# From the first block to the second attention: a first token block sent ahead, bias and gate rows issued sooner, value products and later blocks moved

## The reference

```python
# layer 0, feed-forward: one expert pair for the whole sequence
pooled = ln(x).mean(axis=1)
gate = softmax(pooled @ gate_w.T); top_w, top_i = top_k(gate, 2); top_w /= top_w.sum() + 1e-8
h = gelu(ln(x) @ down_w[top_i].T + down_b[top_i]) * top_w
x = x + h @ up_w[top_i] + (top_w * up_b[top_i]).sum()
# layer 1, attention over 64 anchors, 16 heads of 64
a    = softmax(ln(x) @ W_qk.T @ W_anchor.T / 8)          # tokens x 16 x 64
out  = (a.T @ v) / a.sum(tokens)                         # 16 x 64 x 64
x    = x + (a @ out) @ W_out.T + b_out
```

## Time and profile before

| | |
|---|---|
| runs, median (lowest, highest) | 721.29 us (720.11, 721.71) |
| the profiled execution | 719.99 us, span 718.3 us |
| TensorE busy share, mean granted clock | 97 %, 0.999 |
| VectorE, GpSimd, ScalarE busy share | 81 %, 78 %, 64 % |
| stages around the change, us from the span's start | feed-forward 0 some 475 to 500, attention 1 some 501 to 576 |

### The profile page before, as it was taken

One profiled execution on the slowest core, in us unless ns is written; L12 is line 12 of the kernel. 1 busy time (PEld: TensorE's weight loads), 2 busy tenths in 40 slices (PEclk: granted clock), 3 DMA queues, 4 the chain that ended last, 5 costly groups with the idle time before them and its releaser, 6 DMA issues.

```text
span 718.3 us, 12481 instructions
## 1 busy us (share of the span) xinstructions
PE 698.3 (97%) x4280; PEld 470.6 (66%) x4280; DVE 582.4 (81%) x1213; ACT 460.3 (64%) x1069; POOL 563.6 (78%) x466
## 2 busy tenths in 40 slices
PE   8999999999999999999999999999899999999997
PEld 7665556566566566566666656476566599778885
DVE  8878888988988898898889888756978536878885
ACT  4357776776776777767767766655677822465553
POOL 6468999999999999999999997415688761446674
PEclk9999999999999999999999999999999999999999
DMA  6313768778678688687687683040000000032431
GB/s 152 93 38 67 146 126 155 132 137 151 124 148 150 116 154 153 113 156 146 121 153 139 133 155 67 1 121 2 1 2 0 2 1 1 1 89 81 141 104 30
DMA packets 42595, 68.34 MB, mean 95 GB/s; under 512 B 14872, under 2 KB 24105, under 8 KB 38692
## 3 DMA queue, kind: packets, MB, share of 16 engines
q0 software_dynamic: 15680, 52.96, 38.8%
q1 hardware_dynamic: 25572, 14.47, 7.6%
q10 hardware_dynamic: 1280, 0.12, 0.1%
HBM read 13.35 MB, written 1.10 MB: 20 GB/s over the span
## 4 chain that ended last, share of the span: by engine, by line
PE 71%; POOL 11%; issue 7%; DVE 7%; DMA 3%; ACT 2%; POOLq 0%; ACTq 0%; DVEq 0%
PE ps L1540 16%; PE ps L1584 15%; PE ps L1526 15%; POOL hid_lo L1055 5%; PE ps L1953 4%; PE ps L1568 4%; POOL nrm L1035 2%; DVE mx L1109 2%; PE ps L1993 2%; PE ps L1995 2%; PE ps L1994 2%; POOL hid L1035 1%; DMA w_v<-prob 1%; PE ps L1604 1%; PE ps L1513 1%
## 5 line engine op out<-in xcount | busy, mean ns | idle before, releaser
L1109 DVE TENSOR_REDUCE mx<-ps 128x1 f32<-128x512 f32 x492 | 303.1, 682 | 47.9 <-PE ps L1526 47.8
L658 ACT ACTIVATE prob<-ps 128x512 f32<-128x512 f32 x512 | 261.8, 627 | 21.3 <-PE ps L1540 16.2
L1540 PE MATMUL ps<-q_cols,key 128*128 128x512 f32 x512 | 210.3, 414 | 2.3 <-ACT prob L658 1.7
L1526 PE MATMUL ps<-key,q_rows 128*128 128x512 f32 x512 | 202.8, 400 | 0.8 <-DVE key L1095 0.4
L1540 PEld LDWEIGHTS ps<-q_cols,key 128*128 128x128 f32 x512 | 95.4, 187 | 73.9 <-issue 34.1
L1584 PE MATMUL ps<-prob,val 128*32 128x512 f32 x1024 | 123.3, 598 | 0.0
L1526 PEld LDWEIGHTS ps<-key,q_rows 128*128 128x128 f32 x512 | 95.7, 188 | 18.8 <-DVE mx L1103 1.4
L960 POOL TENSOR_TENSOR pair<-prob 128x512 f32<-128x512 f32 x60 | 104.8, 1770 | 4.0 <-ACT prob L658 4.0
L946 POOL TENSOR_TENSOR part<-prob 128x512 f32<-128x512 f32 x64 | 96.5, 1820 | 5.7 <-ACT prob L658 5.6
L1055 POOL TENSOR_TENSOR hid_lo<-hid,hid_hi 128x512 fp32r<-128x512 f32 x44 | 61.6, 1409 | 38.6 <-ACT hid_hi L826 38.6
L1584 PEld LDWEIGHTS ps<-prob,val 128*32 128x32 f32 x1024 | 26.7, 109 | 51.1 <-issue 47.4
(11 more groups left out here) (301 smaller groups left out, 1319.4 us busy)
## 6 DMA issues: line engine op xcount, KB each, us to landing
part<-prob POOLq DMA_DIRECT2D x16, 1024.0 KB, 7.1
part<-part POOLq DMA_DIRECT2D x14, 512.0 KB, 8.1
w_v<-prob POOLq DMA_DIRECT2D x7, 1024.0 KB, 7.1
hn<-prob POOLq DMA_DIRECT2D x7, 1024.0 KB, 7.0
part<-part POOLq DMA_DIRECT2D x14, 256.0 KB, 7.4
w_v<-w_v POOLq DMA_DIRECT2D x7, 512.0 KB, 8.0
hn<-hn POOLq DMA_DIRECT2D x7, 512.0 KB, 8.0
g_all<-g_rows SPq DMA_DIRECT2D x9, 256.0 KB, 3.2
```

The source lines that it names most:

```text
L658: act.activation(prob[:, g % RING, :], ps[:, g % 3, :], ACT.Exp, scale=SCALE).then_inc(s_exp, 1)
L1109: dve.tensor_reduce(mx[:, n % 2, c % TPB, at:at + 1], ps[:, BANK["rows", 2 * lin + j], :], AX.X, ALU.max).then_inc(s_mrd, 1)
L1526: pe.matmul(ps[:, BANK["rows", 2 * lin + j], :], q_rows[:, k, i * P:(i + 1) * P], key[:, h % KBUF, c0:c0 + BLK], start=True, stop=True).th ...
L1540: pe.matmul(ps[:, g % 3, :], key[:, n // NB % KBUF, t * P:(t + 1) * P], q_cols[:, n % NB, :], start=True, stop=True).then_inc(s_sc, 1)
```

## The change

On PE the group of 8 idle products ahead of the pooled sum is replaced by `values1(0)` and `values1(1)`; the group r = 2 takes the place that r = 0 had between the gate products, and r = 3 stands behind `hidden(3)`. The products for the gate row and for `top_w` are issued ahead of `hidden(0)`, that for the bias row right behind it, and `hidden(1)` goes behind `up(0)`. `ln1_T(0)` goes ahead of `up(2)`, and `up(3)`, `ln1_T(1)` and `ln1_T(2)` go into the loop. ACT copies `top_w` where DVE did, copies `bias0` before it scales `sel_uT`, and makes `ln1_norm(2)`, `ln1_act(1)` and so on inside the loop's turns. DVE normalises block 0 right behind its statistics, and takes `stream0(3)` and the subtractions of blocks 1, 2 and 3 behind turns 0, 1 and 2. POOL's list is as before, and so are the semaphores that the u = 0 slot waits for.

```diff
-        V_BANK = (1, 3, 2, 3)
+        V_BANK = (3, 1, 2, 3)
-        AT_TW = D + E
+        AT_TW = P + 2 * C
@@ ScalarE @@
                 anchors_hi(1)
+                values1(0)
+                values1(1)
                 act.wait_ge(s_gv, 2)
...
                 ln0_act(act, 3, 4)
+                values1(2)
                 act.wait_ge(s_sd_ps, 1)
                 act.copy(sel_dT[:, :], ps[:, 3, 0:P]).then_inc(s_sdT, 1)
-                values1(0)
                 act.wait_ge(s_gb_ps, 1)
                 act.copy(gb[:, :], ps[0:E, 0, AT_GB:AT_GB + P]).then_inc(s_gbc, 1)
+                act.copy(top_w[:, :], ps[:, 0, AT_TW:AT_TW + 1]).then_inc(s_tw, 1)
                 act.wait_ge(s_selb, 1)
                 hidden(0)
+                act.wait_ge(s_b0_ps, 1)
+                act.copy(bias0[:, :], ps[:, 0, AT_BIAS:AT_BIAS + D]).then_inc(s_b0, 1)
+                act.wait_ge(s_su_ps, 2)
                 act.wait_ge(s_tw, 1)
                 act.activation(sel_uT[:, :], ps[:, 2, 0:D], ACT.Copy, scale=top_w[:, :]).then_inc(s_suT, 1)
-                act.wait_ge(s_b0_ps, 1)
-                act.copy(bias0[:, :], ps[:, 0, AT_BIAS:AT_BIAS + D]).then_inc(s_b0, 1)
                 hidden(1)
                 hidden(2)
                 hidden(3)
+                values1(3)
+                ln1_act(act, 0, T1_BANK[0])
                 act.activation(warm[:, :], ones_row[:, 0:1], ACT.Exp)
-                values1(1)
-                ln1_act(act, 0, T1_BANK[0])
                 ln1_norm(act, 1)
-                values1(2)
-                ln1_act(act, 1, T1_BANK[1])
-                ln1_norm(act, 2)
-                values1(3)
-                ln1_act(act, 2, T1_BANK[2])
                 for t in range(NT + LAG1):
                     if t == 1:
+                        ln1_norm(act, 2)
+                        ln1_act(act, 1, T1_BANK[1])
+                    elif t == 2:
                         ln1_norm(act, 3)
-                    elif t == 2:
+                        ln1_act(act, 2, T1_BANK[2])
+                    elif t == 3:
                         ln1_act(act, 3, T1_BANK[3])
@@ VectorE @@
                 anchors_lo(0)
-                dve.wait_ge(s_tw_ps, 2)
-                dve.tensor_copy(top_w[:, :], ps[:, 2, AT_TW:AT_TW + 1]).then_inc(s_tw, 1)
                 anchors_lo(1)
                 stream0(0)
+                ln1_norm(dve, 0)
                 stream0(1)
-                ln1_norm(dve, 0)
+                ln1_lo(dve, 0, T1_BANK[0])
                 stream0(2)
-                ln1_lo(dve, 0, T1_BANK[0])
-                stream0(3)
-                ln1_lo(dve, 1, T1_BANK[1])
...
-                    if t == 1:
+                    if t == 0:
+                        stream0(3)
+                    elif t == 1:
+                        ln1_lo(dve, 1, T1_BANK[1])
+                    elif t == 2:
                         ln1_lo(dve, 2, T1_BANK[2])
                         ln1_lo(dve, 3, T1_BANK[3])
@@ TensorE @@
                 anchor_weights(1)
-                spin(8, 6)
+                pe.wait_ge(s_wo, 2)
+                pe.wait_ge(ln0["hT"], NB + 3)
+                values1(0)
+                values1(1)
                 pe.wait_ge(ln0["hn"], 2 * NT)
...
                 ln0_pe(pe, 3, 4)
-                pe.wait_ge(s_wo, 2)
-                value(0, 0)
-                value(0, 1)
+                value(2, 0)
+                value(2, 1)
...
-                value(0, 2)
-                value(0, 3).then_inc(s_wv_ps, 1)
+                value(2, 2)
+                value(2, 3).then_inc(s_wv_ps, 1)
                 spin(2, 6)
-                pe.wait_ge(ln0["hT"], NB + 3)
+                pe.wait_ge(s_wv, 1)
...
                 last.then_inc(s_sd_ps, 1)
+                pe.wait_ge(s_wv, 3)
...
                 last.then_inc(s_su_ps, 1)
+                pe.wait_ge(s_gv, 10)
+                pe.matmul(ps[0:E, 0, AT_GB:AT_GB + P], g8[:, IDX, :], ones_row[:, :], start=True, stop=True)
+                for k in range(2):
+                    last = pe.matmul(ps[k * BN:(k + 1) * BN, 0, AT_TW:AT_TW + 1], ones_row[:, 0:BN], g1[:, 5 + k:6 + k], start=True, stop=True)
+                last.then_inc(s_gb_ps, 1)
                 pe.wait_ge(s_sdT, 1)
                 hidden(0)
+                pe.wait_ge(s_tw, 1)
+                pe.matmul(ps[:, 0, AT_BIAS:AT_BIAS + D], gb[:, :], up0_b[:, :], start=True, stop=True).then_inc(s_b0_ps, 1)
                 pe.wait_ge(s_selb, 1)
                 pe.wait_ge(s_upx, 1)
...
+                last.then_inc(s_su_ps, 1)
-                hidden(1)
                 pe.wait_ge(s_suT, 1)
                 up(0)
+                hidden(1)
                 hidden(2)
                 up(1)
                 hidden(3)
-                values1(1)
+                values1(3)
+                ln1_T(0)
                 up(2)
-                ln1_T(0)
-                up(3)
-                values1(2)
-                ln1_T(1)
-                pe.wait_ge(s_wv, 1)
                 pe.wait_ge(s_b0, 1)
                 for t in range(NT + LAG1):
                     if t == 1:
-                        values1(3)
+                        up(3)
+                        pe.wait_ge(s_wv, 4)
+                    elif t == 2:
+                        ln1_T(1)
                         ln1_T(2)
-                        pe.wait_ge(s_wv, 4)
                     elif t == 3:
                         ln1_T(3)
```

More of the change, by code:

```diff
@@ L387, in build_kernel @@
         s_oh_ps, s_pick, s_sd_ps, s_sdT, s_su_ps, s_suT, s_selb = (sem(n) for n in ("s_oh_ps", "s_pick", "s_sd_ps", "s_sdT", "s_su_ps", "s_suT", "s_selb"))
-        s_tw_ps, s_tw, s_gb_ps, s_gbc, s_b0_ps, s_b0, s_xb = (sem(n) for n in ("s_tw_ps", "s_tw", "s_gb_ps", "s_gbc", "s_b0_ps", "s_b0", "s_xb"))
+        s_tw, s_gb_ps, s_gbc, s_b0_ps, s_b0, s_xb = (sem(n) for n in ("s_tw", "s_gb_ps", "s_gbc", "s_b0_ps", "s_b0", "s_xb"))
         s_h0_ps, s_h0, s_y0_ps, s_x2 = sem("s_h0_ps"), sem("s_h0"), sem("s_y0_ps"), sem("s_x2")
@@ L1798, in values1 @@
                 def values1(r):
[L1800 to L1805, removed]
                     for q in range(4):
@@ L1870, in _ @@
                 last.then_inc(s_su_ps, 1)
+                pe.wait_ge(s_gv, 10)
[3 more added lines that the diff above has]
+                last.then_inc(s_gb_ps, 1)
                 pe.wait_ge(s_sdT, 1)
                 hidden(0)
-                pe.wait_ge(s_gv, 10)
-                pe.matmul(ps[0:E, 0, AT_GB:AT_GB + P], g8[:, IDX, :], ones_row[:, :], start=True, stop=True).then_inc(s_gb_ps, 1)
+                pe.wait_ge(s_tw, 1)
+                pe.matmul(ps[:, 0, AT_BIAS:AT_BIAS + D], gb[:, :], up0_b[:, :], start=True, stop=True).then_inc(s_b0_ps, 1)
                 pe.wait_ge(s_selb, 1)
@@ L1878, in _ @@
                     last = pe.matmul(ps[:, 2, 0:D], masks[j], up_x[:, j, :], start=(j == 0), stop=(j == E // 2 - 1))
-                for k in range(2):
-                    pe.matmul(ps[k * BN:(k + 1) * BN, 2, AT_TW:AT_TW + 1], ones_row[:, 0:BN], g1[:, 5 + k:6 + k], start=True, stop=True).then_inc(s_tw_ps, 1)
-                hidden(1)
-                pe.wait_ge(s_gbc, 1)
-                pe.matmul(ps[:, 0, AT_BIAS:AT_BIAS + D], gb[:, :], up0_b[:, :], start=True, stop=True).then_inc(s_b0_ps, 1)
+                last.then_inc(s_su_ps, 1)
                 pe.wait_ge(s_suT, 1)
                 up(0)
+                hidden(1)
                 hidden(2)
```

## The result

| | before | changed |
|---|---|---|
| median of 7 runs each (lowest, highest) | 720.44 us (719.39, 721.93) | 723.15 us (722.7, 724.56) |
| ratio, 95 % interval | | 1.0033 (1.0017 to 1.005) |
| span of the profiled execution | 718.3 us | 721.0 us |
| mean granted clock of PE, profiled execution | 0.999 | 0.995 |

The kernel became slower by 0.2 to 0.5 %: 2.4 us by the ratio, 2.7 by the two medians and by the two profiled executions. The forecast was +1.9, and 723.2 us for the median. Behind the numbers that agree stand other parts: +1.1 comes from the new order, less than forecast, and +1.65 from PE's clock, a rival that the prediction had given 6 in 100.

The account below looks back on a forecast made before the run. PE hardly waits from tile 1's slot (517.65) on, so only that start counts; the parts moved it to 519.6, +1.95, tile 2 +1.9. On the median, 721.29 + 1.9 = 723.2 us; 8-in-10 range 720.6 to 725.2.

Parts of the forecast that it names:

- Part 1: Value products replacing PE's spins: pooled sum and gate search start 0.40 us later, bounds 0 and 0.8.
- Part 2: Gate and bias rows: bias row 1.6 us sooner, DVE's add only 0.7 us sooner, bounds 0.3 and 1.1.
- Part 3: DVE normalising block 0 at once: stands still 1.45 us, then meets POOL's bias add; ends 496.83 instead of 497.55.
- Part 4: Into the loop: late half sum and lo of blocks 2 and 3 put tile 0's slot at 515.55, not 511.52.
- The sum: Tile 1's slot 4.04 us behind tile 0's, at 519.6 against 517.65; +1.9 us on the whole kernel.
- the three gaps: PE idle some 7 us in all, ahead of `ln1_T(2)`, `ln1_T(3)` and the slot of tile 0.
- (a): Rival: same order, without the value products' 0.4 or with DVE ahead of POOL (-0.9); +0.6 to +1.4 us; chance 0.29.
- (b): Rival, faster: only DVE's own work counts, last lo before 513.4; -0.5 to -1.4 us; chance 0.15.
- (c): Rival: PE's clock falls to 1.2 GHz in the new gaps, costing 2 to 4 us, 726; chance 0.06.
- (d): Bias row not sooner, as PE waits for group 2's copy; 0.5 us, 723.7; counted within the forecast's 0.50.

Follow-up runs that it names:

- e1: Changed kernel with all four blocks back in the order of before, gate and bias rows still sooner; median 721.32 us, ratio 1.0012.
- e4: Changed kernel, POOL's bias add of block 2 ahead of block 0's rstd, that of block 3 behind block 1's rstd; median 722.82 us, ratio 1.0031.
- e9: Changed kernel with POOL's half sum of tile 0 ahead of the rstd of block 3; median 721.96 us, ratio 1.0017.
- e3: Changed kernel with the wait of tile 0's slot for all four lo split by bank; median 721.12 us, ratio 1.0009.
- e2: Kernel before, with only DVE's lo of blocks 2 and 3 moved behind turn 2 instead of turn 1; median 724.42 us, ratio 1.0043.
- e5: Changed kernel with idle products in PE's three new gaps; median 721.68 us, ratio 1.002.
- e7: Changed kernel with DVE's normalisation of block 0 back behind stream0(1); median 723.10 us, ratio 1.0022.

## Why the prediction was right, and where it was not

Right in direction, in place and in the number, but that the number agrees to 0.05 us (723.2 against 723.15) is luck: three errors cancel. The median of before that it started from, 721.29 of three runs, is 0.85 above the 720.44 of seven; the order's price was put 0.8 too high (+1.9 for +1.1); and the clock's 1.65 is not in the sum.

- **Part 1, the value products**: mis-sized. The chain of waits has the sixteen passes at 1.64 us (`478.88 1.64 PE ps L1799 x16`), not 2.19, against 1.79 of the spins; pooled came at 481.57, not 0.4 later than 481.54. The price is 0, the lower end of its bounds.
- **Part 2, the rows**: the copy of the bias row ended at 489.24 (forecast 489.13), `up(0)` started at 489.96 behind 0.46 us of waiting for `sel_uT`, as said. DVE's add began at 491.16, a gain of 0.98 where 0.72 was forecast: of the 0.4 that part 1 did not cost, 0.26 arrived. By e1 this gain, about 1.0, reaches the end undiminished when the rest is left alone.
- **Part 3, the normalisation**: right. Standing still 1.47 (1.45 forecast), the group 2.06 (2.05), and POOL, whose add started at 494.45, 0.06 us ahead of DVE, won: 1289 ns for the first instruction. The lock by whoever issues first, which the Trainium skill states on the page "SBUF — State Buffer", section "Who interferes with whom", agrees with it. e4 put its price at 0.95.
- **Part 4, the half sum and the four lo**: right in mechanism. cen(0) 503.21 (503.77), cen(1) 507.36 (508.17), half sum 506.99 (507.72), second reciprocal 513.50 (514.15), last lo 514.64 (515.40), tile 0 514.74 (515.55): each 0.56 to 0.81 early. Only 0.26 of this is the earlier start. The rest is an error of the adding: the durations were set end to end, but in the timeline DVE starts the next instruction before the last one's end, so that a block took 1.78 from start to start (496.49 to 498.27) where 1.88 was added, and tmax with cen 2.40 (500.73 to 503.13) where 2.5 was. e9 shows the half sum's share (1.0 at tile 0), e3 and e2 that of the wait for all four.
- **The sum**: tile 0 to tile 1 was set at 4.04, and took 5.69. This is the step that failed. The prediction named the three gaps and their sizes (2.2 to 2.4 each; measured 2.58, 0.81 and 2.14 of idle time) and wrote that they were larger than any before, but took from one gap of 1.94 without a fall that the clock would most likely hold, and put its price into a rival at 6 in 100 instead of into the sum. e5 gives the price, 1.65. All seven runs of the changed kernel have a mean clock of 0.997 or less; of the kernel before, 18 of 33 have 0.998 or more.
- **The rivals**: (a) was half true, for the 0.4 of part 1, and its place in the time, +0.6 to +1.4, is where +1.1 would have come, had the clock held. (b) needed the last lo before 513.4; it came at 514.64. (c) came true in a smaller size (1.65 instead of 2 to 4), and on top of the forecast, not in its place: I had treated as an alternative what is an addition. (d) did not come: no wait for the copy of group 2 is seen.

## What to carry to other kernels

When work is moved out of a prologue into a loop, look up which wait asks for all of it at once; a wait for "all four" makes the last piece's place the only one that counts, and splitting it by what each consumer needs (here by bank) gave back 2.95 us. When a schedule opens gaps on TensorE, add the clock's price to the forecast, as a term and not as a rival; that a gap of 1.94 us did no harm in one execution said nothing of gaps of 2.1 and 2.6. Here GpSimd made the operand that VectorE waited for and started its next instruction 0.06 us ahead of it, and VectorE's first instruction took 1289 ns instead of some 340: such an instruction is better put into the wait ahead (0.95 us in e4). And check a forecast that came true part by part: here it did so by errors that cancel.

## What the runs showed of the hardware that was not expected

- TensorE's clock fell to 1.2 GHz at about 515.7, with the engine at work again, after a stretch in which no gap was longer than 2.58 us, the gaps adding up to 5.5 us between 503.4 and 514.74; in the kernel before one of 1.94 us was without effect in the profiled execution.
- The same gaps can do both: e9, with 2.58, 2.13 and 1.12 us, kept the clock in its profiled execution, and e4, with 2.58, 2.12 and 1.08, lost it at about 510.9. And in e7 it fell at about 483.7 with no gap above 0.25 us in the 19 us ahead. What decides was not found.
- A product of 64 rows cost less in one place than in another: in the chain of waits 16 passes of L1799 take 1.64 us at 478.88 after the change, and 8 passes of the same product (L1796) 1.09 at 499.43 before it. Why was not tried.
